# A fused normalise-project-contract-Fourier kernel: the first phase's VectorE and GpSimd steps placed two units further ahead of TensorE

## What is computed

```python
xn = _ln(_gn(x), norm_w, norm_b)               # over all tokens, then over 64 channels
left = (xn @ left_w + left_b) * mask * sigmoid(xn @ lgate_w + lgate_b)
right = (xn @ right_w + right_b) * mask * sigmoid(xn @ rgate_w + rgate_b)
out_gate = sigmoid(xn @ ogate_w + ogate_b)
...
out = einsum('bkjd,bkid->bijd', left, right)   # then a norm, a product, the gate, + x
...
x = x + _L1_conv_ref(_gn(x), w_real, w_imag)   # 12 x 12 modes of an FFT
```

## Time and profile before

| | us |
|---|---|
| median of 3 runs | 3049.51 |
| the profiled execution, its own time | 3050.38 |
| its span | 3048.6 |
| `project`, from the start of value(0) to the start of value(255) | 247.15 to 1115.16 |
| mean granted TensorE clock over the span | 0.95 of 2.4 GHz |

### The profile page before, as it was taken

One profiled execution on the slowest core, in us unless ns is written; L12 is line 12 of the kernel. 1 busy time (PEld: TensorE's weight loads), 2 busy tenths in 40 slices (PEclk: granted clock), 3 DMA queues, 4 the chain that ended last, 5 costly groups with the idle time before them and its releaser, 6 DMA issues. The chain is left out here.

```text
span 3048.6 us, 40917 instructions
## 1 busy us (share of the span) xinstructions
PE 2516.1 (83%) x12694; PEld 1875.4 (62%) x12694; DVE 2203.9 (72%) x3463; ACT 1373.3 (45%) x1778; POOL 1021.2 (33%) x1042
## 2 busy tenths in 40 slices
PE   0008999989989979999999993889898899789785
PEld 0005666656666648888888882556565666588664
DVE  5997888778778848898888986667676676326443
ACT  0007888778778866677666672112122122100000
POOL 1018888778778820000000000344444444300000
PEclk9999999999999989999999996899999999769998
DMA  9845888887878766777777773999999999849999
GB/s 375 341 182 203 316 318 313 305 309 287 301 298 297 289 269 254 283 287 276 278 281 282 288 276 103 381 373 382 379 386 366 376 389 374 266 162 382 419 419 406
DMA packets 260650, 950.26 MB, mean 312 GB/s; under 512 B 31153, under 2 KB 31665, under 8 KB 260146
## 3 DMA queue, kind: packets, MB, share of 16 engines
q1 hardware_dynamic: 226160, 877.25, 76.2%
q10 hardware_dynamic: 34370, 71.54, 6.1%
HBM read 540.83 MB, written 407.90 MB: 311 GB/s over the span
## 5 line engine op out<-in xcount | busy, mean ns | idle before, releaser
L652 DVE SCALAR_TENSOR_TENSOR pj_lr<-pj_v_ps,layer_b_val,pj_sig 128x1024 f32<-128x1024 f32 x256 | 328.7, 1284 | 163.2 <-ACT pj_sig L589 162.7
L1104 POOL TENSOR_TENSOR fi_square_sum<-fi_square_sum,fi_square 128x1024 f32<-128x1024 f32 x128 | 302.8, 2366 | 424.7 <-ACT fi_square L1075 424.7
L780 PE MATMUL ct_acc_ps<-ct_l_hi,ct_r_hi 128*128 128x512 f32 x1024 | 406.2, 397 | 20.6 <-ACT ct_l_hi L794 20.6
L781 PE MATMUL ct_acc_ps<-ct_l_lo,ct_r_hi 128*128 128x512 f32 x1024 | 405.9, 396 | 0.0
L782 PE MATMUL ct_acc_ps<-ct_l_hi,ct_r_lo 128*128 128x512 f32 x1024 | 405.9, 396 | 0.0
L1075 ACT ACTIVATE fi_square<-fi_x 128x1024 f32<-128x1024 f32 x128 | 135.4, 1058 | 596.0 <-DVE fi_x L1132 583.9
L490 POOL TENSOR_TENSOR front_ring<-front_ring,layer_gn_shift 128x512 f32<-128x512 f32 x256 | 331.2, 1295 | 40.3 <-DVE front_ring L618 40.3
L1031 PE MATMUL fi_y_ps<-fi_scaled,layer_w_bd 128*128 128x512 f32 x512 | 280.7, 631 | 65.5 <-DVE fi_scaled L1115 65.4
L1115 DVE TENSOR_TENSOR fi_scaled<-fi_m,fi_s_ps 128x512 f32<-128x512 f32 x256 | 174.3, 681 | 191.0 <-DMA fi_m<-mixed_d 166.0
L589 ACT ACTIVATE pj_sig<-pj_g_ps,layer_b_gate 128x1024 f32<-128x1024 f32 x256 | 285.6, 1116 | 42.6 <-PE pj_g_ps L555 37.4
L1302 PE MATMUL la_ps_ps<-la_col,la_inv_cols 128*128 128x256 f32 x1024 | 242.9, 400 | 50.1 <-DVE la_early L1372 28.5
(11 more groups left out here) (183 smaller groups left out, 4979.9 us busy)
## 6 DMA issues: line engine op xcount, KB each, us to landing
lr_d<-pj_lr SPq DMA_DIRECT2D x128, 1024.0 KB, 5.4
gate_d<-pj_gout SPq DMA_DIRECT2D x128, 512.0 KB, 6.8
ct_l<-lr_d SPq DMA_DIRECT2D x64, 1024.0 KB, 7.0
ct_r<-lr_d SPq DMA_DIRECT2D x64, 1024.0 KB, 9.0
mixed_d<-ct_o SPq DMA_DIRECT2D x64, 1024.0 KB, 5.0
fi_m<-mixed_d SPq DMA_DIRECT2D x128, 512.0 KB, 14.2
fi_g<-gate_d SPq DMA_DIRECT2D x128, 512.0 KB, 13.3
fi_x<-in_x SPq DMA_DIRECT2D x32, 2048.0 KB, 9.4
```

The source lines that it names most:

```text
L652: dve.scalar_tensor_tensor(out=out[:, :, RG * (m % 2):RG * (m % 2) + RG], in0=v_ps[:, :].rearrange("p (q i) -> p q i", i=RG), scalar=keep. ...
L780: pe.matmul(bank, high, l_hi[b][:, :, k, :], start=(k == 0), stop=False)
L781: pe.matmul(bank, high, l_lo[b][:, :, k, :], start=False, stop=False)
L1104: pool.tensor_tensor(square_sum[:, :, :], square_sum[:, :, :], square[:, :, :], ALU.add).then_inc(sum_done, 1)
```

## The change

All of VectorE's and GpSimd's steps ahead of TensorE move two units further ahead, with the slots of `first_guess` and `newton` moved to match (they now fall in slots m % 8 = 0 and m % 8 = 1, 2, 3). `value(n)`, TensorE's, ScalarE's and SyncE's lists stay as they are. The two engines start two slots earlier.

```diff
-LEAD = 16
+LEAD = 18
...
             def slot(n, m, j):
-                if (m + 5) % UB < 3:
-                    if inside(n + 5):
-                        newton(blocks_before(n, m, j, 5), (m + 5) // UB % 2, (m + 5) % UB)
-                if inside(n + 3):
-                    normalise(n + 3, m + 3, blocks_before(n, m, j, 3))
-                if inside(n + 15):
-                    shift(n + 15, m + 15)
+                if (m + 7) % UB < 3:
+                    if inside(n + 7):
+                        newton(blocks_before(n, m, j, 7), (m + 7) // UB % 2, (m + 7) % UB)
+                if inside(n + 5):
+                    normalise(n + 5, m + 5, blocks_before(n, m, j, 5))
+                if inside(n + 17):
+                    shift(n + 17, m + 17)
...
             def slot(n, m, j):
-                if inside(n + 16):
-                    scale(n + 16, m + 16, rounds_before(n, m, j, 16, UB * RING))
-                if inside(n + 13):
-                    measure(n + 13, m + 13, blocks_before(n, m, j, 13))
-                    if (m + 13) % UB == UB - 1:
-                        first_guess(n + 13, blocks_before(n, m, j, 13), (m + 13) // UB % 2)
+                if inside(n + 18):
+                    scale(n + 18, m + 18, rounds_before(n, m, j, 18, UB * RING))
+                if inside(n + 15):
+                    measure(n + 15, m + 15, blocks_before(n, m, j, 15))
+                    if (m + 15) % UB == UB - 1:
+                        first_guess(n + 15, blocks_before(n, m, j, 15), (m + 15) // UB % 2)
                 if inside(n):
                     value(n, m, j)
```

## The result

The changed kernel took **3025.15 us** (median of 4, 3016.1 to 3029.29) against 3049.59: ratio 0.9917, interval 0.9901 to 0.9933. It is faster, as forecast, but by 24 us where 43 were forecast, and it lies above the range's end of 3019. The profiled execution took 3029.29 us (span 3027.5), the longest of the four.

A forecast was written before the change was run, and what follows sets the result against it. TensorE's pace, 3.11 us a unit, was taken as the bound, with losses to normalise waits and loop returns. -47.8 + 2 + 2.7 = -43.1 us from 3050.38 gave 3007 us, range 3001 to 3019.

The forecast's parts named there:

- The normalise waits, -47.8 us: TensorE's transposes waiting for GpSimd's normalise: with two units more lead all these waits go, -47.8 us.
- The guess in an ordinary block, +2: first_guess in another VectorE slot of each block can make value late for TensorE: +2 us, bounds 0 and 12.7.
- The returns' own loss stays: At the loop's four returns, VectorE's 5.08 us stall and the low clock behind it were to remain unchanged.
- 2.7 for the guess: At the loop's four returns, first_guess now sits between VectorE's stall and value: 4 x 0.67 = +2.7 us, bounds 0 and 4 x 1.6.
- Rival 3: Loop code lies elsewhere in VectorE's and GpSimd's lists; one more stall per return, 20 us: 3028; one less, 2987. Chance 0.05.
- The start, 0: Before value(0), two more scales and measures and the second block's guess fit VectorE's idle time: cost 0, bounds 0 to 1 us.
- The load, 0: SyncE's block load, needed two slots earlier by scale, still has 23.2 us; all 28 landed within 13.2 us: cost 0.

The follow-up runs named there:

- the last experiment: The changed kernel with one small VectorE instruction (128x64 float32) behind value in each unrolled slot 20 to 59, ten each of four forms; no kernel time given.

## Why the prediction was wrong

**The normalise waits, -47.8 us: right.** They went from 89.6 to 9.4 us, and the blocks are 24.90 and 24.95 us. With the returns' stalls out of both kernels the lead is worth 52.5 us, the guess's +2 included. 47.8 was less because the pause at each return hid some of the waits: without it they are 99.1 us in 123 places, 54.8 by the prediction's own sum.

**The guess in an ordinary block, +2: about right.** Without the return stalls the waits for `value` are 7.8 us, 2.1 of them at the start, so 5.7; the kernel before had 3.0 without its stalls. That is 2.7 more.

**"The returns' own loss stays", plus 2.7 for the guess: this is the step that failed.** Comparing kernels with and without the stalls, the four returns cost 868.01 - 847.05 = 21.0 us before and 841.64 - 794.53 = 47.1 us after: 26.1 more, where I had put 2.7. (By the eight blocks around the returns alone it is 20.8 and 45.6, so 24.8 more; the other 1.5 us of the 47.1 stand in the first block, 26.33 against 24.77.) So the phase got -52.5 + 26.1 = -26.4 us, where -43.1 was forecast. At the first return value(96) came 571.74 - 563.98 = 7.76 us after value(95) before, and 12.86 after (546.57 to 559.43). Of the 5.1 us between them, the first stall was 0.46 longer; 3.55 is the second stall, which used to stand behind value(96) at 0.93 and now stands ahead of it; and the remaining 1.1 is the guess with its handoffs, where 0.67 was forecast. My bound for this term, 4 x 1.6, took the second stall for something that keeps its size and its slot. It keeps its place in the list.

**The rivals.** Rival 3, to which I gave 0.05, is what happened, in its sum (+20 was written, and 3028) though not in its form: no stall was added, one that had been covered by VectorE's own work was uncovered. "The loop's code lies elsewhere" was its reason, and that holds: two prologue slots are ten instructions, and they moved the head from 16 to 6 ahead of the border. The page cited there goes further than I used it. The Trainium skill, Runtime: NRT & Kernel Launch, Instruction fetch mechanics, has code refilled in blocks of 256 instructions, two of which are held on most engines. 963 + 256 = 1219: the loops that begin at 947 to 962 and end at 1251 to 1269 lie in three blocks, those that begin at 965 or 966 in two. By that rule the last are free, and the runs agree (no idle issue time at VectorE's first instructions of a pass, no instruction packet on queue 14 from 555 to 945 us).

On the size of a fetch the trace differs, and it decides: the packets of queue 14 hold 8 KB, and the unrolled kernel, whose lists of VectorE, GpSimd, ScalarE and SyncE are together 2,471 instructions longer than those of the kernel with eight small ones, has 19 more of them. That makes some 130 instructions a packet, not 256. After the first return of the changed kernel they come at 559.0, 602.3 and 642.9 us, 0.8 to 3.5 us after VectorE reached places 963, 1091 and 1219 (about 558.2, 598.8 and 641.1 us), which are 128 apart. The border at 963 is shown by the loops that begin at 947, 957 and 962 on one side and at 965, 966 and 997 (the kernel of the last experiment) on the other. How many fetched pieces an engine holds is not shown, and the lists of the other engines weren't moved across a border of theirs.

**The start, 0: wrong, +2.05.** I counted the guess at 0.67 us from a row in which GpSimd stood still. Ahead of value(0) it is at work, and the guess took 3.5 us. In the five kernels with the guess ahead of it value(0) starts at 249.1 to 249.2, in the six others at 246.2 to 247.2. Moving the guess behind value(0) gave some 1.6 us by value(8).

**The load, 0: right.** Its 28 landed in 13.3 us at most, against 23.2 there were.

**Left open.** The part behind value(255), which the edits don't touch, took 1931.7 to 1943.6 us over the profiles of this case. That scatter, and 3.3 us of the difference between the two first profiles, I can't explain. Nor is it shown why a fetch takes some 5 us; the DMA engines were busy to a share of 1.00 and 0.97 through the first stall of the first return, before and after, and whether a fetch would be shorter without that traffic isn't shown.

## What to carry to other kernels

The price of a hardware loop can depend on where it begins, as it did for the 305 to 308 instructions of VectorE's here. Count the engine's list up to the head. Look for idle time without a cause at the first instructions of a pass, and count the instruction packets in the profile's list of DMA queues. Eight small instructions ahead of the loop were worth more here (47 us) than the change that was tried (24 us). Any edit ahead of a loop can win or lose by chance: ten such instructions in the kernel before cost 12 us, eighteen saved 16. When a change is judged by its time, compare blocks away from the returns as well. For lateness of a producer with enough throughput, the lead needed can be read off one timeline: 1.85 us late, one slot of 3.11 us enough.

## What the runs showed that I had not expected

- A loop of 308 instructions on VectorE returns with no stall when it begins at place 965 of the list, and with 9.62 us when it begins at 962. Where both waits stand apart, VectorE idles 4.4 to 5.6 us before the first instruction of a pass, and the instruction at place 963 starts 4.8 to 5.1 us after that one, over the sixteen returns of four kernels.
- The profile counts these fetches: 60 instruction packets on queue 14 in the five kernels whose returns stall, 40 in the five with a loop that doesn't.
- A VectorE tensor_scalar of 0.2 us with its operands in SBUF lasted up to 1.4 us while GpSimd ran a tensor_tensor, and ended some 0.05 us behind it; a tensor_tensor of the same size with one operand in PSUM stayed within 205 to 211 ns.
